# w2's four weight blocks asked for by ScalarE at 8 KB a row, in place of SyncE at 2 KB a piece

## The chip, the cores and the metric

One Trainium2 chip, one core. The metric is the device time of one execution in microseconds; three runs of the kernel before are at hand and one profiled execution. TensorE is the matmul engine (PE in the profile, PEld its weight loads), VectorE is DVE, ScalarE is ACT, GpSimd is POOL, and SyncE (SP, SPq for its DMA queue) issues transfers.

## What is computed

Cross attention over 32 sequences of 128 rows with 512 features, and then a feed-forward block with ternary weights (512 to 2048 and back), both with residuals. Cut to what matters:

```python
x = x + xattn(layernorm(x), ctx, mask)      # scores, softmax, readout with ctx
h = layernorm(x)
# bitlinear: xq = act_quant(rms_norm(h)); wq = weight_quant(w); xq @ wq.T + b
def weight_quant(w):
    scale = 1.0 / clip(mean(abs(w)), 1e-05)
    return clip(round(w * scale), -1, 1) / scale
h = gelu(silu(bitlinear(h, w1, b1)))         # 128 x 2048 for each sequence
h = layernorm(h) * g + b
x = x + bitlinear(h, w2, b2)                 # w2: 512 x 2048
```

The scale of a weight matrix is the mean of the absolute values of the whole of it, so w2 must have landed completely before any of it can be rounded, and all of it is needed for the first second product.

## The kernel before, in words

The work is cut into 32 tiles t of 128 rows (one sequence each). Every engine has one program written out by hand as a list of steps, and semaphores tie them together; an engine does its steps strictly in the order of its list. For each tile: SyncE loads x, ctx and both transposed (256 KB each, rows of 2 KB); TensorE makes scores, turns the probabilities and makes the readout; VectorE adds the readout to x; POOL centres and rounds it to fp16 (round_q1, L1575); SyncE turns it with a DMA transpose (transpose_q1, L253 to L257); TensorE makes first_product(t, h) in two halves h (L614 to L631); ScalarE applies silu (L1193) and gelu (L1202) and sums squares; VectorE applies gain and beta; POOL rounds; SyncE transposes again (transpose_q2); TensorE makes second_product (L633); VectorE adds it to x; SyncE stores. Tiles follow one another some six steps apart, so that all engines work on different tiles at a time.

The weights are prepared once, at the start. w1 lies raw in the first four of the eight buffers of hid, w2 in the last four (w2raw, L124): block c is 128 partitions by 2048 floats. The buffers are used by tiles 4 to 7 first, so silu(4) to silu(7) wait until their block has been rounded. For each block c of w2 ScalarE sums the absolute values of one half (weight_sum, L1139) and VectorE those of the other half (L1858). VectorE adds the eight half-sums of wsum up (wtot, L1868), TensorE adds over the partitions (weight_total, L546), VectorE makes the scale (L1870), and then POOL and ScalarE round the blocks into w2q (L1542, L1151), which VectorE clamps (L1893).

The transfers of w2 are asked for by SyncE in load_w2 (L249). w2T is the transposed weight, 2048 x 512, in DRAM, and block c takes four runs of 128 of its rows, so each partition gets four pieces of 2 KB. SyncE's list in this stretch reads (L317 to L332): transpose_q1(0), ctxT(6), ctx(3), **w2(0)**, ctxT(7), x(6), **w2(1)**, transpose_q1(1), **w2(2)**, **w2(3)**, x(7), xT(6), ctx(4), ctx(5), transpose_q1(2). transpose_q1(t) waits for POOL's round_q1(t), and all that is listed behind it waits too. load_ctx(t) waits for readout(t - 2).

```python
            def transpose_q1(t):
                sp.wait_ge(s_q1, t + 1)
                wait(sp, s_z[0], t - 3)
                wait(sp, s_z[1], t - 3)
                sp.dma_start(q1T[:, t % 4, :, :], q1[:, t % 3, :], transpose=True).then_inc(s_q1T[t % 4], 16)
```

ScalarE's list in this stretch (L1241 to L1263): exp_scores(3), copy_b1, round_w1(2), copy_probT(3), mean_term(4), square_x1(2), mean_term(5), exp_scores(4), square_x1(3), weight_sum(1, 0), exp_scores(5), copy_b2, silu(0, 0), copy_probT(4), weight_sum(1, 1), mean_term(6), silu(0, 1), weight_sum(1, 2), copy_probT(5), silu(1, 0), weight_sum(1, 3), silu(1, 1), gelu(0). copy_b1 reads what TensorE's turn_b1 (L551) left.

TensorE's list (L679 to L718): turn_b1, readout(2), turn_b2, warm(5), column_sums(4), turn_probs(3), turn_factors(0), warm(6), readout(3), warm(7), scores(4), which waits for mean_term(5), warm(8), scores(5), turn_probs(4), which waits for exp_scores(4), first_product(0, 0), column_sums(6), first_product(0, 1), turn_factors(1), turn_probs(5), first_product(1, 0), first_product(1, 1), weight_total(1), readout(4). warm(i) are six matmuls on zeros (L539 to L544). VectorE's list has weight_sum(1, 0) to (1, 3) between other steps, and then weight_sums_total(1), x_stats(7), weight_scale(1) (L2057 to L2070).

Of the kernel before, what the change touches and what calls it, by code (L numbers as in the profile page):

```python
# [15 lines left out]
P = 128  # L16
# [22 lines left out]

def build(nc, x_in, xT_in, ctx_in, ctxT_in, mask_in, w1T_in, b1_in, g_in, b_in, w2T_in, b2_in, out):  # L40
    NT, _, D = x_in.shape
    FF = w1T_in.shape[1]
    DC = D // P
    FC = FF // P
    HALF = FF // 2
    CH = 512
# [23 lines left out]
    with ExitStack() as stack:  # L70
# [3 lines left out]
        def sem(name):  # L74
            return stack.enter_context(nc.semaphore(name))
# [48 lines left out]
        w2raw = hid[:, 4:8, 0:FF]  # L124
# [34 lines left out]
        s_w2 = [sem(f"w2_landed{c}") for c in range(4)]  # L159
# [41 lines left out]
        def wait(eng, semaphore, value):  # L201
            if value > 0:
                eng.wait_ge(semaphore, value)
# [12 lines left out]
        def w2_flat(c):  # L216
            return w2q[:, 4 * c:4 * c + 4, :].rearrange("p a d -> p (a d)")
# [5 lines left out]
        def _(sp):  # L223
            def load_x(t):
                if t >= XR:
                    sp.wait_ge(s_out[t % XR], landed(t - XR, XR))
                sp.dma_start(xs[:, t % XR, :], x_in[t, :, :]).then_inc(s_x[t % XR], 16)
# [5 lines left out]
            def load_ctxT(t):  # L233
                wait(sp, s_score, t - CT + 1)
                wait(sp, s_csp, (t - CT) // 2 + 1)
                sp.dma_start(ctxT[:, t % CT, :, :], ctxT_in[t, :, :, :]).then_inc(s_ctxT[t % CT], 16)

            def load_ctx(t):
                wait(sp, s_read, t - CX + 1)
                sp.dma_start(ctx[:, t % CX, :], ctx_in[t, :, :]).then_inc(s_ctx[t % CX], 16)  # L240
# [5 lines left out]
            def load_w1(c):  # L246
                sp.dma_start(w1raw[:, c, :], w1T_in[c * P:(c + 1) * P, :]).then_inc(s_w1[c], 16)

            def load_w2(c):  # L249
                sp.dma_start(w2raw[:, c, :].rearrange("p (c d) -> p c d", d=D),  # L250
                             w2T_in[c * CH:(c + 1) * CH, :].rearrange("(c p) d -> p c d", p=P)).then_inc(s_w2[c], 16)

            def transpose_q1(t):  # L253
                sp.wait_ge(s_q1, t + 1)
                wait(sp, s_z[0], t - 3)
                wait(sp, s_z[1], t - 3)
                sp.dma_start(q1T[:, t % 4, :, :], q1[:, t % 3, :], transpose=True).then_inc(s_q1T[t % 4], 16)  # L257
# [59 lines left out]
            transpose_q1(0)  # L317
            load_ctxT(6)
            load_ctx(3)
            load_w2(0)  # L320
            load_ctxT(7)
            load_x(6)
            load_w2(1)
            transpose_q1(1)
            load_w2(2)
            load_w2(3)
            load_x(7)
            load_xT(6)
            load_ctx(4)
# [806 lines left out]

        @block.scalar
        def _(act):
            def weight_sum(k, c):  # L1139
                raw, s_landed = (w1raw, s_w1) if k == 0 else (w2raw, s_w2)  # L1140
                act.wait_ge(s_landed[c], 16)
                n = FF if c in WHOLE[k] else HALF
                unread = (w1q[:, c, :] if k == 0 else w2_flat(c))[:, 0:n]
                act.activation(unread, raw[:, c, 0:n], ACT.Abs, accum_out=wsum[:, k, c:c + 1]).then_inc(s_wsum[k], n // HALF)

            def round_w1(q):
                act.wait_ge(s_wsc[0], 1)
                cols = slice(q * CH, (q + 1) * CH)
                act.activation(w1q[:, :, cols], w1raw[:, :, cols], ACT.Identity, scale=wscale[:, 0:1]).then_inc(s_w1q[q], 1)
# [5 lines left out]
            def copy_b1():  # L1155
                act.wait_ge(s_bturn[0], 1)
                act.wait_ge(s_zero, 2)
                act.activation(rows1[0:ROWS, :], b1_ps, ACT.Copy).then_inc(s_rows[0], 1)
# [6 lines left out]
            def exp_scores(t):  # L1165
                wait(act, s_pTp, t - 3)
                act.wait_ge(s_centred, t + 1)
                act.activation(prob[:, t % 4, :], score[:, t % 4, :], ACT.Exp, bias=nbias[:, t:t + 1],
                               scale=-1.0, accum_out=psum_p[:, t:t + 1]).then_inc(s_prob, 1)

            def mean_term(t):

                act.wait_ge(s_csp, t // 2 + 1)
                act.wait_ge(s_mv1, t + 1)
                wait(act, s_centred, t - CR + 1)
                act.activation(corr[:, t % CR, :], csum_ps[:, t % 2 * P:(t % 2 + 1) * P], ACT.Identity,
                               scale=mv1[:, t, 0:1]).then_inc(s_corr, 1)

            def copy_probT(t):
                act.wait_ge(s_pTp, t + 1)  # L1180
                wait(act, s_read, t - 1)
                act.activation(probT[:, t % 2, :], probT_ps, ACT.Copy).then_inc(s_turn, 1)  # L1182

            def square_x1(t):
                if t == 0:
                    act.wait_ge(s_const, 1)
                act.wait_ge(s_xc, t + 1)
                wait(act, s_sq2, t)

                act.activation(junk_x[:, :], xc[:, t % 3, 0:D + 2], ACT.Square, scale=ROOT1,  # L1190
                               accum_out=sq2[:, t:t + 1]).then_inc(s_sq2, 1)
# [33 lines left out]
            mean_term(0)  # L1225
            mean_term(1)
            weight_sum(0, 0)
            exp_scores(0)
            copy_probT(0)
            exp_scores(1)  # L1230
            mean_term(2)
            copy_probT(1)
            mean_term(3)
            weight_sum(0, 1)
            weight_sum(0, 2)
            weight_sum(0, 3)
            exp_scores(2)
            square_x1(0)
            copy_probT(2)
            square_x1(1)  # L1240
            exp_scores(3)  # L1241
            copy_b1()
            round_w1(2)
            copy_probT(3)
            mean_term(4)
            square_x1(2)
            mean_term(5)
            exp_scores(4)
            square_x1(3)
            weight_sum(1, 0)  # L1250
# [1240 lines left out]
```

## Time and profile before

| | us |
|---|---|
| median of 3 runs (lowest, highest) | 420.21 (418.86, 420.68) |
| profiled execution, its own time | 419.71 |
| its span | 417.9 |
| busy: TensorE matmuls, ScalarE, VectorE, POOL | 385.4, 381.7, 365.9, 274.7 |
| DMA: all transfers | 73.87 MB, 64.7% of 16 engines' span in SyncE's queue |
| w2: four transfers of 1024 KB, median from issue to landing | 7.9 |

Busy time is the sum of an engine's instructions; an idle engine costs something only where it is on the chain that sets the end. In the page's slices DMA moves 274 to 411 GB/s in the first 63 us (six slices) and mostly 50 to 250 after. All plain loads and transposes are issued by SyncE, in one queue.

### The profile page before, as it was taken

To read this page: it belongs to the slowest core of one execution; us is meant where nothing else is said; L and a number is where in the kernel's file an instruction comes from. 1 tells how busy PE (TensorE), PEld (TensorE's weight loads), DVE (VectorE), ACT (ScalarE), POOL (GpSimd) and SP (SyncE) were. 2 spreads that over 40 slices of the span, in tenths; PEclk is the share of its full clock that TensorE was granted. 3 is DMA by queue.
4 is the path that set the end of the run, shared out by engine and by line. 5 is a ranking of instruction groups with operands and counts; after the bars stand their busy time and mean duration, and the time that the engine had idled before them with its cause. 6 is when DMAs were issued, how large, how long until landed. Compare 5 with 4: busy or idle time off the path is not lost.

```text
span 417.9 us, 6814 instructions
## 1 busy us (share of the span) xinstructions
PE 385.4 (92%) x1878; PEld 205.5 (49%) x1878; DVE 365.9 (88%) x571; ACT 381.7 (91%) x517; POOL 274.7 (66%) x373
## 2 busy tenths in 40 slices
PE   3999987899999999999999999999999987899896
PEld 2677353544455544544545455554545433444342
DVE  5278579989999989999999999989998689999992
ACT  1496999999999999999999999999999999999960
POOL 6358488774687838664785569499368855477930
PEclk9999998699999999999999999999999996999999
DMA  7999991556665787658568766594654423083484
GB/s 274 411 343 303 368 340 50 163 152 143 202 151 134 183 188 191 138 168 199 152 169 248 191 166 160 190 217 118 176 129 105 91 63 63 2 201 102 88 214 128
DMA packets 110389, 73.87 MB, mean 177 GB/s; under 512 B 87048, under 2 KB 87056, under 8 KB 109584
## 3 DMA queue, kind: packets, MB, share of 16 engines
q1 hardware_dynamic: 110352, 73.43, 64.7%
q8 instruction: 16, 0.26, 0.3%
q14 instruction: 21, 0.17, 0.1%
HBM read 44.05 MB, written 8.39 MB: 125 GB/s over the span
## 4 chain that ended last, share of the span: by engine, by line
issue 24%; PE 21%; ACT 20%; DVE 16%; POOL 13%; DMA 4%; DVEq 0%; POOLq 0%; SPq 0%; ACTq 0%
ACT junk_v L1211 6%; PE z L624 6%; DVE hid L1971 5%; DVE hid L1980 5%; PE acc L649 5%; ACT hid L1206 4%; ACT hid L1200 3%; POOL hid L1617 3%; DMA xT<-in_xT_dram 3%; PE ba L574 3%; PE ba L585 3%; POOL rstd L1606 2%; PE bb L599 2%; PE z L629 2%; ACT junk_l L1222 1%
## 5 line engine op out<-in xcount | busy, mean ns | idle before, releaser
L624 PE MATMUL z<-w1q,q1T 128*128 128x512 f16 x512 | 124.2, 386 | 2.8 <-ACT hid L1200 2.6
L649 PE MATMUL acc<-w2q,q2T 128*128 128x512 f16 x512 | 117.3, 379 | 0.4 <-DMA q2T<-hid 0.4
L1980 DVE SCALAR_TENSOR_TENSOR hid<-hid,rstd,beta 128x2048 f32<-128x2048 f32 x32 | 76.6, 2396 | 6.2 <-POOL rstd L1606 5.8
L624 PEld LDWEIGHTS z<-w1q,q1T 128*128 128x128 f16 x512 | 49.8, 99 | 65.2 <-ACT hid L1200 9.4
L1971 DVE SCALAR_TENSOR_TENSOR hid<-hid,nmu,gain 128x2048 f32<-128x2048 f32 x32 | 79.1, 2472 | 0.4 <-POOL nmu L1598 0.3
L649 PEld LDWEIGHTS acc<-w2q,q2T 128*128 128x128 f16 x512 | 49.9, 98 | 58.1 <-DMA q2T<-hid 0.9
L1985 DVE TENSOR_REDUCE am<-hid 128x1 f32<-128x2049 f32 x32 | 72.5, 2269 | 0.1
L1200 ACT ACTIVATE hid<-z,fac 128x1024 f32<-128x1024 f32 x64 | 70.7, 1118 | 0.9 <-PE z L629 0.5
L1222 ACT ACTIVATE junk_l<-hid 128x2050 bf16<-128x2050 f32 x32 | 61.1, 1910 | 3.8 <-DVE hid L1980 3.7
L1211 ACT ACTIVATE junk_v<-hid,gsum 128x2048 bf16<-128x2048 f32 x32 | 63.7, 1990 | 0.1
L1617 POOL TENSOR_SCALAR hid<-hid,kq 128x2048 f16<-128x2048 f32 x30 | 60.9, 2031 | 4.3 <-DVE kq L1992 2.7
L1206 ACT ACTIVATE hid<-hid 128x2048 f32<-128x2048 f32 x32 | 60.9, 1905 | 0.2
L629 PE MATMUL z<-rows,brows 128*128 128x512 bf16 x128 | 38.5, 383 | 1.4 <-DVE brows L1960 1.4
L1575 POOL TENSOR_SCALAR q<-xc,kq 128x512 f16<-128x512 f32 x32 | 36.0, 1124 | 4.9 <-DVE kq L1933 3.0
L574 PE MATMUL ba<-ctxT,xT 128*128 128x128 f32 x256 | 37.8, 293 | 0.4 <-DMA xT<-in_xT_dram 0.4
L585 PE MATMUL ba<-ctxT,neg 128*128 128x256 f32 x128 | 32.3, 398 | 6.1 <-DMA ctxT<-in_ctxT_dram 5.9
L599 PE MATMUL bb<-ctx,probT 128*128 128x512 f32 x64 | 34.0, 613 | 0.8 <-ACT probT L1182 0.5
L1568 POOL TENSOR_TENSOR rho<-sq,c_neghalf 128x2 f32<-128x2 f32 (+1 forms) x17 | 17.1, 1005 | 26.7 <-ACT junk_x L1190 26.7
L574 PEld LDWEIGHTS ba<-ctxT,xT 128*128 128x128 f32 x256 | 32.8, 201 | 3.1 <-issue 1.5
L585 PEld LDWEIGHTS ba<-ctxT,neg 128*128 128x128 f32 x128 | 24.8, 199 | 12.1 <-issue 7.3
L1921 DVE SCALAR_TENSOR_TENSOR xs<-bb,rsum,xs 128x512 f32<-128x512 f32 x32 | 23.8, 744 | 6.5 <-PE bb L599 6.2
L1604 POOL TENSOR_SCALAR ve<-vsum 128x2 f32<-128x2 f32 (+1 forms) x18 | 9.9, 548 | 28.8 <-ACT junk_v L1211 28.4
(105 smaller groups left out, 573.3 us busy)
## 6 DMA issues: line engine op xcount, KB each, us to landing
ctxT<-in_ctxT_dram SPq DMA_DIRECT2D x32, 256.0 KB, 3.7
xs<-in_x_dram SPq DMA_DIRECT2D x32, 256.0 KB, 3.9
xT<-in_xT_dram SPq DMA_DIRECT2D x32, 256.0 KB, 3.5
ctx<-in_ctx_dram SPq DMA_DIRECT2D x32, 256.0 KB, 3.5
out_dram<-xs SPq DMA_DIRECT2D x32, 256.0 KB, 3.1
hid<-in_w1T_dram SPq DMA_DIRECT2D x4, 1024.0 KB, 10.0
hid<-in_w2T_dram SPq DMA_DIRECT2D x4, 1024.0 KB, 7.9
gain<-in_g_dram SPq DMA_DIRECT2D x1, 1024.0 KB, 11.1
```

The costliest lines, as they stand in the source:

```text
L574: mm = pe.matmul(score_ps, xT[:, t % XT, c, :], ctxT[:, t % CT, c, :], start=False, stop=(c == DC - 1))
L585: mm = pe.matmul(csum_ps, neg[:, :], ctxT[:, t % CT:t % CT + 2, c, :], start=(c == 0), stop=(c == DC - 1))
L624: pe.matmul(z_ps[h][:, c * CH:(c + 1) * CH], q1T[:, t % 4, k, :], w1q[:, k, f0:f0 + CH], start=(k == 0), stop=False)
L649: mm = pe.matmul(a, q2T[:, t % 2, c, :], w2q[:, c, :], start=False, stop=(c == FC - 1))
L1200: act.activation(hid[:, t % HR, half(h)], z_ps[h][:, :], ACT.Silu, scale=fac[:, t, 0:1]).then_inc(s_silu[h], 1)
L1206: act.activation(hh, hh, ACT.Gelu, accum_out=gsum[:, t:t + 1]).then_inc(s_gelu, 1)
L1211: act.activation(junk_v[:, :], hid[:, t % HR, 0:FF], ACT.Square, bias=gsum[:, t:t + 1], scale=-float(FF), accum_out=vsum[:, t:t + 1]).then ...
L1222: act.activation(junk_l[:, :], hid[:, row_of(t), 0:FF + 2], ACT.Square, scale=ROOT2, accum_out=ysum[:, t:t + 1]).then_inc(s_sq, 1)
L1617: pool.tensor_scalar(q2_of(t), hid[:, row_of(t), 0:FF], kq2[:, t:t + 1], UNIT, ALU.mult, ALU.mult).then_inc(s_q2, 1)
L1971: dve.scalar_tensor_tensor(out=hid[:, row_of(t), 0:FF], in0=hid[:, t % HR, 0:FF], scalar=nmu[:, t:t + 1], in1=gain[:, :], op0=ALU.add, op1 ...
L1980: dve.scalar_tensor_tensor(out=hh, in0=hh, scalar=rstd[:, t:t + 1], in1=beta[:, :], op0=ALU.mult, op1=ALU.add).then_inc(s_l, 1)
L1985: dve.tensor_reduce(am2[:, t:t + 1], hid[:, row_of(t), 0:FF + 1], AX_X, ALU.max, apply_absolute_value=True).then_inc(s_am2, 1)
```

## The change

load_w2 moves from SyncE's program to ScalarE's, and the host lays w2T out otherwise, so that a partition's 2048 floats of a block lie together in DRAM: a row of 8 KB. What lands in w2raw is the same. SyncE's list loses its four load_w2; in ScalarE's list load_w2(0) stands behind exp_scores(3), load_w2(1) behind round_w1(2), and load_w2(2) and load_w2(3) behind mean_term(5). No wait is added or removed.

```diff
-            def load_w2(c):
-                sp.dma_start(w2raw[:, c, :].rearrange("p (c d) -> p c d", d=D),
-                             w2T_in[c * CH:(c + 1) * CH, :].rearrange("(c p) d -> p c d", p=P)).then_inc(s_w2[c], 16)
...
             load_ctx(3)
-            load_w2(0)
             load_ctxT(7)
             load_x(6)
-            load_w2(1)
             transpose_q1(1)
-            load_w2(2)
-            load_w2(3)
             load_x(7)
...
         def _(act):
+            def load_w2(c):
+                act.dma_start(w2raw[:, c, :], w2T_in[c * P:(c + 1) * P, :]).then_inc(s_w2[c], 16)
+
...
             exp_scores(3)
+            load_w2(0)
             copy_b1()
             round_w1(2)
+            load_w2(1)
             copy_probT(3)
             mean_term(4)
             square_x1(2)
             mean_term(5)
+            load_w2(2)
+            load_w2(3)
             exp_scores(4)
...
-        "w2T": np.asarray(inputs["L0_ffn_w2"]).T,
+        "w2T": np.asarray(inputs["L0_ffn_w2"]).T.reshape(4, FF // 4 // P, P, D).transpose(0, 2, 1, 3).reshape(4 * P, FF // 4 // P * D),
```

## Rows read from the trace of the kernel before

**Rows 1.** ScalarE's windows: stretch, length, busy, granted clock, DMA share, GB/s.
```profile
36.00:100.00 64.00, 62.93 (x92) 0.92 0.73 218
...
300.00:400.00 100.00, 98.86 (x115) 0.97 0.44 98
```

**Rows 2.** TensorE's timeline: start, duration, engine, line, operation, [idle before, releaser].
```profile
24.64 1.13 PE L574 MATMUL ba<-ctxT,xT 128*128 128x128 f32 x8 [0.40 <-DMA xT<-in_xT_dram]
...
32.28 1.02 PE L599 MATMUL bb<-ctx,probT 128*128 128x512 f32 x2
...
33.79 0.22 PE L570 MATMUL ba<-maskb,ones_b 128*128 128x128 bf16 x1
...
42.94 1.89 PE L624 MATMUL z<-w1q,q1T 128*128 128x512 f16 x8
...
47.95 0.35 PE L549 MATMUL acc<-wtot,neg 128*128 128x1 f32 x2 [0.43 <-DVE wtot L1868]
...
68.82 0.23 PE L570 MATMUL ba<-maskb,ones_b 128*128 128x128 bf16 x1 [1.86 <-ACT corr L1176]
...
77.17 3.48 PE L624 MATMUL z<-w1q,q1T 128*128 128x512 f16 x8
```

**Rows 3.** Timeline of ScalarE.
```profile
27.79 1.87 ACT L1158 ACTIVATE rows<-z 9x2048 bf16<-9x2048 bf16 x1 [0.54 <-PE z L555]
...
31.77 0.28 ACT L1182 ACTIVATE probT<-bb 128x128 f32<-128x128 f32 x1 [0.22 <-PE bb L593]
...
35.45 0.40 ACT L1168 ACTIVATE prob<-score,nbias 128x129 f32<-128x129 f32 x1 [2.23 <-DVE nbias L1909]
...
45.46 1.11 ACT L1200 ACTIVATE hid<-z,fac 128x1024 f32<-128x1024 f32 x1
...
47.42 0.19 ACT L1144 ACTIVATION_READ_ACCUMULATOR w2q<-hid 128x1 f32 x1
```

**Rows 4.** Windows, all engines; the last columns are DMA share and GB/s.
```profile
17.00:20.00 3.00, 2.42 (x10) 1.60 (x9) 2.21 (x8) 1.09 (x5) 0.96 (x3) 1.00 1.02 427
...
33.00:36.00 3.00, 3.00 (x26) 2.54 (x25) 2.70 (x8) 0.77 (x4) 2.41 (x5) 1.00 1.07 391
...
37.20:40.30 3.10, 3.10 (x16) 2.09 (x15) 3.10 (x7) 2.43 (x6) 3.10 (x2) 1.00 0.76 118
```

**Rows 5.** Waits of VectorE (36-60 us), ScalarE (100-418): total, times, longest.
```profile
DVE wsum L1862 <- DMA hid<-in_w2T_dram: 2.6, 2, 1.6
...
ACT junk_l L1222 <- DVE hid L1980: 3.7, 6, 2.4
```

**Rows 6.** SyncE's queue: timeline, then line 250's four issues in ns.
```profile
28.83 0.43 SPq L250 DMA_DIRECT2D hid<-in_w2T_dram  x1
...
36.42 1.20 SPq L257 DMA_TRANSPOSE q1T<-q  x1
...
37.67 1.13 SPq L250 DMA_DIRECT2D hid<-in_w2T_dram  x2
...
L250 SPq DMA_DIRECT2D hid<-in_w2T_dram x4: 434/470/582, 27.3 to 38.3; - x4
```

**Rows 7.** Issue to landing: w2(1), q1T(1), then w2(2) and w2(3) together.
```profile
DMA to landing us min/median/max: 10.3/10.3/10.3
...
DMA to landing us min/median/max: 3.9/3.9/3.9
...
DMA to landing us min/median/max: 5.7/6.8/8.0
```

**Rows 8.** Timeline of VectorE.
```profile
47.64 0.16 DVE L1868 TENSOR_REDUCE wtot<-wsum 128x1 f32<-128x8 f32 x1
...
53.62 0.35 DVE L1909 CUSTOM_DVE_ANT_0 score<-corr,ba,nrs 128x128 f32<-128x128 f32 x1 [2.26 <-PE ba L574]
```

**Rows 9.** DMA packets of 37 to 39.2 us.
```profile
DMA packets 635, 0.30 MB, mean 134 GB/s; under 512 B 558, under 2 KB 558, under 8 KB 634
```

**Rows 10.** Window of all engines; granted clock is third from the right.
```profile
72.00:78.00 6.00, 4.73 (x19) 3.30 (x20) 5.95 (x14) 5.97 (x8) 5.48 (x7) 0.50 0.25 64
```

## The prediction

> **What bounds the kernel now.** I read the windows of ScalarE first. From 36 to 100 us it is busy for 62.93 of 64 us, and from 300 to 400 us for 98.86 of 100 [rows 1], so in that time the end is set by the sum of ScalarE's own instructions: a change counts there only if it shifts ScalarE's start or gives it work. Before that the chain of waits lies on TensorE. In its timeline the reader sees no idle time in brackets between 24.64 us (released by xT) and 47.95, where 0.43 us of idle end, so it worked without a gap to 47.52 [rows 2]. It hands over to ScalarE at the first products: silu(1, 0) starts at 45.46 [rows 3], when the product that began at 42.94 and took 1.89 us [rows 2] has added its two bias matmuls. So what moves TensorE between 27 and 47 us moves the whole rest; what moves only VectorE, POOL or DMA in that time does nothing until it reaches TensorE or ScalarE.
>
> DMA looks like a limit too: at 33 to 36 us it moves 391 GB/s with its engines busy throughout [rows 4]. But the only wait for w2 that the profile names is VectorE's: 2.6 us in two times [rows 5].
>
> **The change, part by part.**
>
> *1. w2 lands earlier: worth nothing.* In the old order w2(2) and w2(3) stand in SyncE's program behind transpose_q1(1), which waits for round_q1(1) and issues at 36.42; the pair follows at 37.67 [rows 6] and lands 5.7 and 8.0 us after its issues [rows 7], the second at 46.3. In the new order ScalarE asks for them after mean_term(5), which ended 2.23 us before 35.45, at 33.2 [rows 3]: some 4 us earlier. VectorE's two sums then need not wait. But the next step, wtot at 47.64 [rows 8], needs all eight half-sums, and ScalarE's last one is read out at 47.42 plus 0.19, so 47.61 [rows 3]. It stands behind silu(1, 0), which has nothing to do with w2. So w2's scale comes at the same time, and with it the roundings. Gain: 0.
>
> *2. 8 KB rows in place of 2 KB pieces.* While w1 (8 KB rows) was most of the traffic, 427 GB/s were moved; in the stretch of w2 and x, all in 2 KB pieces, 391 [rows 4]. For w2's 4.19 MB that is 9.8 us of DMA time against 10.7, 0.9 less. Nothing on the path waits for that time, so it pays 0; it only shortens the backlog in term 4. [...]
>
> *3. Four issues on ScalarE.* The trace has no DMA issued by ScalarE. The nearest rows are SyncE's: its four issues of w2 took 0.43 to 0.58 us, and the longest issue near them, the transpose's, 1.20 [rows 6]. The lower bound is 0, if the issue hides beside the instruction before it; nothing below that, since ScalarE loses no instruction. I take 0.5, by the same transfer on the other queue. load_w2(0) stands before copy_b1, which started at 27.79 after 0.54 us of idle time, released by TensorE [rows 3]: 0.54 covers 0.5. load_w2(1) stands before copy_probT(3), which started at 31.77 after 0.22 of idle time [rows 3]; 0.28 is left. readout(3) on TensorE needs probT. It started at 32.28 after warming matmuls [rows 2], while probT was ready at 31.77 + 0.28 = 32.05; now it is ready at 32.33, and with a hand-over of some 0.05 TensorE is 0.1 late. mean_term(5) then ends at 33.5, before scores(4), which waits for it, at 33.79 + 0.1 [rows 2]. load_w2(2) and (3) take 33.5 to 34.5, and exp_scores(4) is not before 35.45 [rows 3]; without that cover they would cost their 1.0 in full. **Cost 0.1.** At 1.20 each: the first overruns its cover by 0.7, the second by 1.0, so probT(3) is ready at 33.7 and TensorE 1.5 late; the last two end near 37.3, and exp_scores(4) is still through before turn_probs(4) wants it. Upper end 1.5.
>
> *4. q1T(1) beside w2.* first_product(1, 0) waits for this transfer. It is issued at 36.42 [rows 6] and lands 3.9 us later, at 40.3 [rows 7]; the product starts at 42.94 without having waited [rows 2]: a slack of 2.6 us. Until now only w2(1) was ahead of it, landed at 28.83 + 10.3 = 39.1 [rows 6, 7]. Now w2(2) and w2(3), 2.1 MB, are in flight from ScalarE's queue on the same engines. Lower bound: the queues share by bytes, q1T(1) keeps most of its slack, 0 late. Upper bound: all of w2 goes first. w2(0) and (1) gain 0.5 by the faster rate, so 38.6; 2.1 MB at 427 GB/s are 4.9, so 43.5; the transpose itself needs about 1.3 more, the better part of the 2.2 us window that holds its packets, 558 small ones in all [rows 9]: 44.8, which is 1.9 late. Between these: the packets alternate. q1T(1) has 512 packets of 256 B, 32 on each of 16 engines; w2(2) and (3) have 16 rows on each, at 8 KB / 26.7 GB/s = 0.31 us. When the transpose arrives, near 37.6, some 14 rows are left: 4.3 us, in which 14 of the 32 go by. The other 18 take 0.5 us and the completion some 0.7: 43.1. I take that, **0.2 late**: it is the case between ends that no row tells apart. [...]
>
> *5. SyncE's queue without w2.* x(7), xT(6), ctx(4) and ctx(5) are issued 1.1 us earlier, since the pair's issues took 1.13 [rows 6], and 2.1 MB no longer stand ahead of them. From 37.2 to 40.3 us DMA moved only 118 GB/s [rows 4]: the transpose ran, and w2(2) was only being started. That hole fills. The first user of these four is readout(4), on TensorE behind 47.52, after the hand-over to ScalarE: 0.
>
> Sum: 0 + 0 + 0.1 + 0.2 + 0 = +0.3. The profiled execution took 419.71 (a span of 417.9 and 1.8 around it), so it would take 420.0. It lies 0.5 below the median of the three runs, 420.21; on that scale the forecast is **420.5**. A measurement of this kernel tells about 0.5% (2.1 us) from no change, and 0.3 lies well within.
>
> **The rivals.**
>
> *A. The transpose starves and TensorE's clock falls (slower).* Place: TensorE at 42.94. [...] The products (1, 0) and (1, 1), both on the path, would cost 1.6 more each: 420.2 + 1.9 + 3.2 = **425.3**. Against: TensorE had not waited for 18 us before 42.94, and 44.8 needs nearly all of w2 ahead. It decides from a landing after 45.0, or from a fall of the clock near 43: 0.12.
>
> *B. Issues on ScalarE are dear.* At 1.20 each +1.5, with term 4 +1.7: **421.9**, within 0.5%. For: it is that queue's first use, beside SyncE's issues until 29.3. Against: none of SyncE's plain w2 issues took over 0.58. 0.08, a quarter of it over the bound.
>
> *C. VectorE's head start reaches the end (faster).* The 2.6 us of waits go, and ScalarE's longest wait for VectorE, late in the kernel, is 2.4 [rows 5]. If all of that went: 420.2 - 2.4 = **417.8**. Against: behind its sums VectorE stops at wtot for ScalarE anyway, and soon after it waits 2.26 us for TensorE until 53.62 [rows 8], so the lead is eaten by then. 0.12.
>
> *D. The change does not do what it says.* w2 in the other queue is served no sooner and no faster, the issues hide, and q1T(1) is on time. Every term is 0: **420.2**. 0.12.
>
> **How the numbers follow.** Forecast 0.56, A 0.12, B 0.08, C 0.12, D 0.12. Same: 0.56 + 0.12 + 0.06 = 0.74. Slower: 0.12 + 0.02 = 0.14. Faster: 0.12. Both upper ends together (1.5 + 1.9) make 423.6; I take 422.7, as they seldom meet. To leave out no more than 2 in 10, the range must take in C, with A left out: 417.7 to 422.7. The likeliest case alone, with the spread of the three runs (418.86 to 420.68), would be 418.9 to 421.5.
>
> **What the changed profile should show.** Four issues on ScalarE's queue near 27.3, 31.6 and 33.5 us, each near 0.5; copy_probT(3) at about 32.0; w2(3) landed at 42 to 43.5, not 46.3; no wait of VectorE for w2, but wtot still at 47.6 to 48; q1T(1) landed at 41 to 43.5, not 40.3; silu(1, 0) at 45.5 to 45.9, and the old timeline behind it, shifted by that. DMA in 37.2 to 40.3 us well above 118 GB/s. The forecast is wrong if silu(1, 0) moves by more than 2 us either way, if the clock drops near 43 us, or if silu(1, 0) stays and the end still moves: then a chain after 48 us counts that I hold to be only shifted.

## The result, and the profile after

The changed kernel is slower, where no measurable difference was forecast.

| | before | after |
|---|---|---|
| median (lowest to highest), 4 runs each | 419.56 (418.86 to 420.68) | 426.94 (425.92 to 428.08) |
| ratio of the two, 95% interval | | 1.0177 [1.0157, 1.0197] |
| profiled execution, and its span | 419.71, 417.9 | 426.55, 424.7 |

426.94 lies outside the range of 417.7 to 422.7. The page of the changed kernel, parts 2 and 3 (q1 is the queue in which SyncE asks, q10 that of ScalarE):

```profile
span 424.7 us, 6814 instructions
...
PEclk9996999999999999999999999999999997999999
...
q1 hardware_dynamic: 108240, 69.24, 61.1%
q10 hardware_dynamic: 576, 4.19, 2.5%
```

All 4.19 MB of w2 now run in q10. TensorE's clock has a dent in the fourth slice, 32 to 42 us. TensorE's timeline there, with the columns of [rows 2]:

```profile
23.65 1.13 PE L566 MATMUL ba<-ctxT,xT 128*128 128x128 f32 x8 [0.55 <-DMA xT<-in_xT_dram]
...
30.57 0.82 PE L536 MATMUL z<-idle 128*128 128x256 bf16 x6
37.09 2.04 PE L591 MATMUL bb<-ctx,probT 128*128 128x512 f32 x2 [5.70 <-DMA ctx<-in_ctx_dram]
38.93 1.49 PE L536 MATMUL z<-idle 128*128 128x256 bf16 x6
40.21 0.31 PE L562 MATMUL ba<-maskb,ones_b 128*128 128x128 bf16 x1
40.31 1.50 PE L566 MATMUL ba<-ctxT,xT 128*128 128x128 f32 x8
...
49.80 1.89 PE L616 MATMUL z<-w1q,q1T 128*128 128x512 f16 x8
```

The reader is to see the 5.70 in brackets: readout(3) waited for **ctx(3)**, a transfer that the prediction never looked at. Before, readout(3) ran at 32.28 without a wait [rows 2]. SyncE's queue in the changed kernel shows the issue, and the view of line 240 from 25.6 to 26 us the time to its landing:

```profile
25.16 0.52 SPq L236 DMA_DIRECT2D ctxT<-in_ctxT_dram  x1
25.72 0.43 SPq L240 DMA_DIRECT2D ctx<-in_ctx_dram  x1
...
DMA to landing us min/median/max: 11.1/11.1/11.1
```

Before, the same two views gave

```profile
26.86 0.43 SPq L240 DMA_DIRECT2D ctx<-in_ctx_dram  x1
...
DMA to landing us min/median/max: 4.3/4.3/4.3
```

so ctx(3) landed at 31.2, 1.1 us before readout(3) wanted it. The chain of work that ended last now runs through this transfer:

```profile
25.72 11.13 DMA ctx<-in_ctx_dram
36.85 0.24 issue
37.09 2.04 PE bb L591 x2
```

**Where the time went.** This run reached scores(3) at 23.65, before at 24.64 [rows 2]. That 0.99 us lies ahead of the first changed issue, so I count from scores(3). readout(3) starts 13.44 us after it (before 32.28 - 24.64 = 7.64): 5.80 later. From readout(3) to first_product(1, 0), at 49.80, it is 12.71 us (before 42.94 - 32.28 = 10.66): 2.05 more. These 2.05 are the matmuls at the low clock (0.57 in 36 to 42 us): readout(3) took 2.04 where it took 1.02 [rows 2], the six warming matmuls 1.49 against 0.82, scores(4) 1.50 against 1.11. The last, before:

```profile
33.85 1.11 PE L574 MATMUL ba<-ctxT,xT 128*128 128x128 f32 x8
```

Together 7.85, less the head start of 0.99: 6.86. Windows of all engines (columns as in [rows 4], the granted clock third from the right):

```profile
31.40:37.10 5.70, 0.01 (x1) 0.04 (x1) 0.88 (x2) 0.75 (x3) 1.24 (x3) 0.75 0.99 396
36.00:42.00 6.00, 4.91 (x21) 3.30 (x22) 1.51 (x4) 0.00 (x0) 1.75 (x3) 0.57 0.83 341
42.00:48.00 6.00, 6.00 (x36) 4.15 (x34) 5.28 (x15) 5.02 (x11) 4.99 (x8) 1.00 0.63 185
```

In the first row TensorE does nothing, while DMA moves 396 GB/s: the wait is not a lack of transfer, but of the one transfer that counts. Then comes a clock of 0.57 (0.50 in [rows 10]), and from 42 us on one of 1.00.

ScalarE's timeline (ACTq is its queue of issues):

```profile
25.22 0.38 ACTq L1132 DMA_DIRECT2D hid<-in_w2T_dram  x1
25.72 0.39 ACT L1163 ACTIVATE prob<-score,nbias 128x129 f32<-128x129 f32 x1
26.74 1.87 ACT L1153 ACTIVATE rows<-z 9x2048 bf16<-9x2048 bf16 x1 [0.54 <-PE z L547]
26.75 0.33 ACTq L1132 DMA_DIRECT2D hid<-in_w2T_dram  x1
28.52 1.99 ACT L1144 ACTIVATE w1q<-hid,wscale 128x2048 f16<-128x2048 f32 x1
30.72 0.28 ACT L1177 ACTIVATE probT<-bb 128x128 f32<-128x128 f32 x1 [0.21 <-PE bb L585]
31.27 0.82 ACTq L1132 DMA_DIRECT2D hid<-in_w2T_dram  x2
42.30 0.40 ACT L1163 ACTIVATE prob<-score,nbias 128x129 f32<-128x129 f32 x1 [10.14 <-DVE nbias L1908]
...
52.22 1.11 ACT L1195 ACTIVATE hid<-z,fac 128x1024 f32<-128x1024 f32 x1
```

exp_scores(4) waited 10.14 us where it waited 2.23, and silu(1, 0) starts at 52.22, before at 45.46 [rows 3]: +6.76. I followed ScalarE's later table loads to the end (ACT_TABLE_LOAD in the trace, 1.28 us each, at its exp, silu and gelu; every kernel here has 17, 17 and 13 of them on the same three steps): each of the 47 is 6.7 to 6.9 us late, and the span is 6.8 longer. So all of the loss arises between 31 and 43 us, and nothing is won back or lost behind it.

**Why ctx(3) was late.** The packets of 29 to 31 us, by queue (packets, MB, share), in the changed kernel:

```profile
DMA packets 159, 0.83 MB, mean 413 GB/s; under 512 B 0, under 2 KB 0, under 8 KB 79
...
q10 hardware_dynamic: 79, 0.65, 77.9%
q1 hardware_dynamic: 79, 0.16, 21.3%
```

and in the kernel before, same stretch:

```profile
q1 hardware_dynamic: 381, 0.71, 102.0%
```

The queues got the same number of packets, 79 each, but one of q10 is an 8 KB row and one of q1 a 2 KB row: the bytes are split four to one. SyncE's queue fell from 0.71 MB in 2 us (w2's own pieces included) to 0.16. Everything in it suffered: ctxT(6) took 8.5 us (before 4.2), ctxT(7) 13.7 (8.0), x(6) 16.2 (8.3). Of these, ctx(3) had the least slack.

### The profile page after: what moved, and what is told of

Read it like the earlier page. It is cut to its first block, busy times and chain, and to the rows that moved or that the text cites. A ratio compares the mean times of both kernels' runs of the same rounds, so it can differ in the third digit from the quotient of the medians.

```text
span 424.7 us, 6814 instructions
## 1 busy us (share of the span) xinstructions
PE 381.4 (90%) x1878; PEld 203.3 (48%) x1878; DVE 366.1 (86%) x571; ACT 381.6 (90%) x517; POOL 269.7 (64%) x373
## 3 DMA queue, kind: packets, MB, share of 16 engines
q10 hardware_dynamic: 576, 4.19, 2.5%
## 4 chain that ended last, share of the span: by engine, by line
issue 23%; ACT 21%; DVE 20%; PE 19%; POOL 9%; DMA 4%; SPq 2%; DVEq 0%; POOLq 0%; ACTq 0%
ACT junk_v L1206 6%; DVE hid L1979 6%; DVE hid L1970 5%; PE z L616 5%; PE acc L641 5%; ACT hid L1201 4%; ACT hid L1195 4%; PE ba L566 3%; POOL hid L1616 3%; DMA ctx<-in_ctx_dram 3%; DVE am L1984 2%; PE bb L591 2%; POOL rstd L1605 2%; PE z L621 1%; DVE st L1898 1%
## 5 line engine op out<-in xcount | busy, mean ns | idle before, releaser
L616 PE MATMUL z<-w1q,q1T 128*128 128x512 f16 x512 | 122.6, 383 | 3.7 <-ACT hid L1195 3.7
L566 PE MATMUL ba<-ctxT,xT 128*128 128x128 f32 x256 | 36.2, 285 | 1.6 <-DMA xT<-in_xT_dram 1.6
L1574 POOL TENSOR_SCALAR q<-xc,kq 128x512 f16<-128x512 f32 x32 | 33.8, 1057 | 4.9 <-DVE kq L1932 3.0
L1920 DVE SCALAR_TENSOR_TENSOR xs<-bb,rsum,xs 128x512 f32<-128x512 f32 x32 | 23.8, 743 | 12.9 <-PE bb L591 12.8
L566 PEld LDWEIGHTS ba<-ctxT,xT 128*128 128x128 f32 x256 | 31.5, 194 | 4.3 <-issue 2.9
L1561 POOL TENSOR_SCALAR xc<-xs,sum 128x512 f32<-128x512 f32 x32 | 26.2, 818 | 9.9 <-DVE xs L1920 9.5
L577 PEld LDWEIGHTS ba<-ctxT,neg 128*128 128x128 f32 x128 | 24.8, 199 | 12.9 <-issue 8.2
L1567 POOL TENSOR_TENSOR rho<-sq,c_neghalf 128x2 f32<-128x2 f32 (+1 forms) x17 | 13.7, 804 | 26.8 <-ACT junk_x L1185 26.8
```

Of the source, the lines that this page charges most:

```text
L566: mm = pe.matmul(score_ps, xT[:, t % XT, c, :], ctxT[:, t % CT, c, :], start=False, stop=(c == DC - 1))
L577: mm = pe.matmul(csum_ps, neg[:, :], ctxT[:, t % CT:t % CT + 2, c, :], start=(c == 0), stop=(c == DC - 1))
L616: pe.matmul(z_ps[h][:, c * CH:(c + 1) * CH], q1T[:, t % 4, k, :], w1q[:, k, f0:f0 + CH], start=(k == 0), stop=False)
```

## The experiments

My theory behind the result: the two queues take turns by packets (79 to 79 in 29 to 31 us), so the 8 KB rows in the second queue (0.65 MB) starve the 2 KB transfers of the first (0.16 MB); the wait of 5.70 us for ctx(3) does the rest, with the clock of 0.57 behind it. The rivals: it is the second queue as such, whatever its rows (E1); it is the 8 KB rows as such (E2); the fall of the clock is the greater part of it (E5). Each group ran beside the kernel before on the same chip, whose median was 419.57 for E1 to E4, 419.53 for E5 to E8, 419.28 for E9 to E11 and 419.50 for E12. The ratios are made from runs taken in the same rounds, so they can differ by 0.1 or 0.2% from the quotient of two medians.

**E1. ScalarE's queue and places, but the old layout in 2 KB pieces.**

```diff
-                act.dma_start(w2raw[:, c, :], w2T_in[c * P:(c + 1) * P, :]).then_inc(s_w2[c], 16)
+                act.dma_start(w2raw[:, c, :].rearrange("p (c d) -> p c d", d=D),
+                              w2T_in[c * CH:(c + 1) * CH, :].rearrange("(c p) d -> p c d", p=P)).then_inc(s_w2[c], 16)
```

> The changed kernel, w2 still asked for by ScalarE at the same places, but in pieces of 2 KB as before. Theory P (the two queues take turns packet by packet, so a queue of 2 KB rows gets a fifth of the bytes beside one of 8 KB rows): with equal pieces SyncE's queue gets half, ctx(3) lands near 32 us instead of 36.8, readout(3) waits some 0.6 us instead of 5.7, and the time is +0.3 to +1.5 us on the kernel before. Rival V (w2 is simply asked for too early, its 1 to 2 MB stand ahead whatever their rows): ctx(3) still lands after 35 us and the time stays at +6 to +8.

Measured: 424.08 (423.52 to 425.56), ratio 1.0091 [1.006, 1.0122]. ctx(3) landed 8.1 us after its issue. TensorE's timeline:

```profile
36.51 2.05 PE L591 MATMUL bb<-ctx,probT 128*128 128x512 f32 x2 [2.71 <-DMA ctx<-in_ctx_dram]
```

The wait is 2.7 and not 0.6, and the clock fell here as well (2.05); the time is 4.5 us above the kernel before, three times the upper end of my expectation and below that of the rival. So the rows carry part of the loss. A good half stays without them. It can't be put down to the second queue alone, since w2 is asked for early here too: w2(0) at 27.60, ahead of ctx(3) at 28.21, while in the kernel before w2(0) stood behind ctx(3). E6 takes the second queue away. The packets by queue in this kernel, first 30 to 33 us, then 33.5 to 36:

```profile
q10 hardware_dynamic: 401, 0.82, 74.6%
q1 hardware_dynamic: 162, 0.30, 27.8%
...
q10 hardware_dynamic: 260, 0.50, 53.7%
q1 hardware_dynamic: 255, 0.46, 49.8%
```

From 33.5 us on the queues got nearly the same number of packets, with equal rows and so nearly equal bytes (0.50 and 0.46 MB). Before that SyncE's queue, which had just come out of the transpose of q1(0), got less than its half (162 of 563 packets). Why is open; my expectation had the fair half throughout. (The profiled execution took 425.56, 1.5 above the median.)

**E2. SyncE's queue and old places, but 8 KB rows.** (The host layout is that of the change.)

```diff
-                sp.dma_start(w2raw[:, c, :].rearrange("p (c d) -> p c d", d=D),
-                             w2T_in[c * CH:(c + 1) * CH, :].rearrange("(c p) d -> p c d", p=P)).then_inc(s_w2[c], 16)
+                sp.dma_start(w2raw[:, c, :], w2T_in[c * P:(c + 1) * P, :]).then_inc(s_w2[c], 16)
```

> The kernel before with only the layout changed: SyncE asks for w2 at the old places, at 8 KB a row. Theory P: in one queue nothing takes turns, ctx(3) lands as before (near 31 us), w2(1) some 0.5 to 0.9 us sooner, nothing on the path moves: -0.3 to +0.5 us. Rival R (8 KB rows hold the engines up by themselves): +3 or more.

Measured: 419.57 (10 runs), ratio 0.9988 [0.9969, 1.0006]. ctx(3) took 4.4 us and nothing waited for it. VectorE's waits for w2 sank from 2.6 [rows 5] to

```profile
DVE wsum L1861 <- DMA hid<-in_w2T_dram: 1.5, 2, 1.2
```

and the end did not move. By themselves, in SyncE's queue and places, the 8 KB rows were harmless and worth nothing here. The gain in rate of term 2 is not clear either. w2(0) and w2(1) landed 7.8 and 10.3 us after their issues, before 7.9 and 10.3; w2(2) and w2(3) took 5.0 and 6.9, before 5.7 and 8.0. From 33 to 36 us DMA moved 394 GB/s, before 391 [rows 4], and from 31.5 to 35.5 us 419, before 389.

**E3. The changed kernel, with w2(0) and w2(1) asked for behind mean_term(4).**

```diff
             exp_scores(3)
-            load_w2(0)
             copy_b1()
             round_w1(2)
-            load_w2(1)
             copy_probT(3)
             mean_term(4)
+            load_w2(0)
+            load_w2(1)
```

> The changed kernel with load_w2(0) and (1) moved behind mean_term(4), so that they are issued near 31 us and not at 25.2 and 26.8. Theory P: ctx(3), ctxT(6), ctxT(7) and x(6) are through before w2 begins, readout(3) does not wait; next q1T(1) takes turns with w2 and lands near 42.5, some 0.6 after it is wanted: 0 to +1.5 us. Rival I (issuing on ScalarE costs by itself, wherever it stands): +5 or more.

Measured: 423.78 (421.76 to 424.61), ratio 1.0083 [1.0055, 1.0111]. ctx(3) took 5.8 us, and readout(3) waited 0.30. (w2 was asked for at 32.13, so it was not beside ctx(3). Why that took 1.5 us longer than before is open, and shows how much such a landing can vary.) So this loss went, and the next one came, far larger than the 0.6 that I expected: q1T(1), issued at 37.16, took 9.1 us, and first_product(1, 0) waited for it:

```profile
46.39 3.36 PE L616 MATMUL z<-w1q,q1T 128*128 128x512 f16 x8 [2.47 <-DMA q1T<-q]
```

Eight matmuls that take 1.89 took 3.36: the clock fell, to 0.58 in 46.4 to 50 us. This is rival A, place and mechanism, with the low clock over one product and not two. ScalarE's issues, asked for where nothing covers them, also left 0.52 us of idle time here; exp_scores(4) behind them waited 2.19 for VectorE anyway, so nothing shows that it reached the end:

```profile
33.10 0.63 ACT L1185 ACTIVATE junk_x<-xc 128x514 bf16<-128x514 f32 x1 [0.52 <-issue]
```

**E4. The changed kernel, with ctx(3) asked for earlier.**

```diff
             load_xT(5)
+            load_ctx(3)
             load_ctxT(5)
             load_x(5)
             transpose_q1(0)
             load_ctxT(6)
-            load_ctx(3)
```

> The changed kernel with load_ctx(3) moved up in SyncE's list, behind xT(5). Theory P: readout(3) no longer waits, but SyncE's queue is as starved as before: ctxT(7), x(6) and q1T(1) still land near 40, 43 and 44 us, wanted at 38, 38.6 and 42, and the wait comes back at column_sums(6) or at the first products: +3 to +5 us. Rival S (only ctx(3) was short of time, all else has slack): 0 to +1 us.

Measured: 422.01 (10 runs), ratio 1.0057 [1.0033, 1.0082]. readout(3) did not wait, and 4.9 of the 7.4 us are gone. The 2.4 that stay lie between the rival's 0 to 1 and my 3 to 5. This is the direct test: w2 runs as in the changed kernel, and only ctx(3) is out of its way. What is left shows as waits for the other transfers in SyncE's queue: x(6) landed 14.3 us after its issue, and VectorE waited 2.4 for it; q1T(1) took 7.4. TensorE's timeline:

```profile
43.87 1.89 PE L616 MATMUL z<-w1q,q1T 128*128 128x512 f16 x8 [0.46 <-DMA q1T<-q]
...
46.12 0.60 PE L621 MATMUL z<-rows,brows 128*128 128x512 bf16 x2 [0.36 <-DVE brows L1959]
```

**E5 and E10. The changed kernel, with eight more groups of warming matmuls before readout(3)**, so that the clock stays up during the wait. They write what nothing reads. E10 is E5 again.

```diff
             warm(6)
+            warm(6)
...
+            warm(6)
             readout(3)
```

> The changed kernel with eight more groups of six warming matmuls in front of readout(3), some 5.3 us of TensorE's time, which lie inside its wait of 5.7 us. [...] Rival: the matmuls after the wait are not on the path, or the clock falls all the same; then +6.5 to +8.

> The same kernel as in e5_warm. There the first product began 1.7 us earlier after its start than in the changed kernel, yet the time was not shorter. Theory (the clock's fall costs its 1.7 us): 1 to 2 us below e9_again. Rival (what is saved before 48 us is lost again later): within 0.7 us of e9_again, with ScalarE's lag on the kernel before growing after 100 us in the trace.

Measured: 427.27 (426.87 to 427.39), 1.0188 [1.016, 1.0215]; again 426.98 (424.93 to 429.93), 1.0188 [1.0153, 1.0223]. The clock stayed up, in E5 (1.00 from 31 to 38 us):

```profile
37.86 1.10 PE L591 MATMUL bb<-ctx,probT 128*128 128x512 f32 x2 [0.67 <-DMA ctx<-in_ctx_dram]
```

first_product(0, 0) came 18.18 us after the start of scores(3), 1.75 earlier than in the changed kernel. Yet the time, for which I had forecast 1.5 to 2.2 us below the changed kernel, did not shrink, and 7.7 above the kernel before lies in the rival's range. In that run ScalarE's lag behind the kernel before grew from 5.5 us to 6.5 by 278 us, in steps near 110 and 278 us. In E10 there was little to keep: ctx(3) itself took 12.9 us, readout(3) waited 2.28 behind the warming matmuls, and first_product(0, 0) came 20.26 us after scores(3), against 20.65 in E9; the lag then grew from 8.1 to 9.4. The lag of the changed kernel stays at 6.7 to 6.8, but E9's grew too, by 0.3 us, so not all of such growth belongs to the warming. The six times of E10 lie 5 us apart. What the fall of the clock costs in the end is therefore not settled: 2.05 us in the trace, nothing in the medians. That it is the greater part of the loss is refuted.

**E6. All in SyncE's queue at 8 KB, w2(0) and w2(1) moved ahead**, so that ctx(3) has w2 before it without any second queue.

```diff
             transpose_q1(0)
+            load_w2(0)
             load_ctxT(6)
             load_ctx(3)
-            load_w2(0)
+            load_w2(1)
             load_ctxT(7)
             load_x(6)
-            load_w2(1)
             transpose_q1(1)
```

> All of w2 in SyncE's queue at 8 KB a row, but asked for as early as ScalarE does it: w2(0) ahead of ctxT(6) and ctx(3), w2(1) behind ctx(3), (2) and (3) at the old places. Theory P (turn-taking between queues): one block ahead in one queue costs its own transfer time, 2.5 us; ctx(3) lands near 33.7 counted from the same start, readout(3) waits about 1.5 us, perhaps with a fall of the clock: +1.5 to +3.5. Rival V (the early request is the cost, in whichever queue): +6 or more.

Measured: 423.47 (422.25 to 423.74), ratio 1.0089 [1.0054, 1.0125]. ctx(3) took 7.2 us.

```profile
34.76 1.34 PE L598 MATMUL bb<-ctx,probT 128*128 128x512 f32 x2 [2.33 <-DMA ctx<-in_ctx_dram]
```

A loss needs no second queue: one block ahead of ctx(3) in its own queue gives a wait of 2.3 us, more than the 1.5 I expected, a fall of the clock (readout(3) took 1.34, before 1.02) and +3.9 us, a little above my +3.5. That is as much as E1 lost. So an early request alone accounts for about half of the 7.4 us, in either queue. The other half came only with the second queue and 8 KB rows together. It is a question of which bytes go ahead of ctx(3).

**E7. The changed kernel, in rows of 4 KB** (two pieces for each partition, and a host layout to suit).

```diff
-                act.dma_start(w2raw[:, c, :], w2T_in[c * P:(c + 1) * P, :]).then_inc(s_w2[c], 16)
+                act.dma_start(w2raw[:, c, :].rearrange("p (h d) -> p h d", d=2 * D),
+                              w2T_in[2 * c * P:2 * (c + 1) * P, :].rearrange("(h p) d -> p h d", p=P)).then_inc(s_w2[c], 16)
```

> The changed kernel with w2's rows cut into two pieces of 4 KB, asked for by ScalarE at the same places. Theory P: SyncE's 2 KB rows get a third of the bytes, between a half (2 KB pieces, readout(3) waited 2.7 us) and a fifth (8 KB rows, 5.7 us): a wait of 3.5 to 5 us and +5 to +7. Rival (the size of the pieces does nothing, 2.7 and 5.7 differ by chance of timing): a wait near 2.7 or near 5.7.

Measured: 424.75 (422.55 to 425.6), ratio 1.0121 [1.0082, 1.0161]. ctx(3) took 8.9 us. TensorE's timeline, and the packets of 31 to 35 us:

```profile
35.29 1.10 PE L591 MATMUL bb<-ctx,probT 128*128 128x512 f32 x2 [3.40 <-DMA ctx<-in_ctx_dram]
```

```profile
q10 hardware_dynamic: 278, 1.07, 67.9%
q1 hardware_dynamic: 272, 0.50, 33.4%
```

Equal counts once more, and bytes two to one. In the profiled execution, which took 422.55, 2.2 below the median, the clock did not fall in spite of a wait of 3.4 us (it was 1.00 in 31.9 to 35.3 us). With E1 and the changed kernel the row size makes a series: at 2, 4 and 8 KB ctx(3) took 8.1, 8.9 and 11.1 us, readout(3) waited 2.7, 3.4 and 5.7, and the ratios are 1.0091, 1.0121 and 1.0177. The step from 4 to 8 KB is clear. That from 2 to 4 KB is not: the two intervals overlap, and at 8 KB alone four traces gave 11.1, 11.3, 11.3 and 12.9 us.

**E8. w2(0) and w2(1) in SyncE's queue in their old places, w2(2) and w2(3) in ScalarE's, all at 8 KB.** SyncE gets a load_w2 of its own again. This leaves ctx(3) alone and gives q1T(1) the two blocks that the prediction feared.

```diff
             load_ctx(3)
+            load_w2(0)
             load_ctxT(7)
             load_x(6)
+            load_w2(1)
             transpose_q1(1)
...
             exp_scores(3)
-            load_w2(0)
             copy_b1()
             round_w1(2)
-            load_w2(1)
             copy_probT(3)
```

> Half of the change undone: w2(0) and (1) in SyncE's queue at the old places, at 8 KB a row; w2(2) and (3) asked for by ScalarE behind mean_term(5). Theory P: ctx(3) is on time, near 31 us, and readout(3) does not wait; but the transpose of q1T(1), 32 packets of 256 B on each engine, takes turns with the rows of w2(2) and (3) and lands near 43.5 to 44.5 instead of 40.3: first_product(1, 0) waits 0.5 to 2 us: +0.5 to +3. Rival S (only ctx(3) was short of time): -0.5 to +0.5.

Measured: 420.91 (420.57 to 421.5, 10 runs), ratio 1.0035 [1.0023, 1.0047]. ctx(3) took 4.6 us. q1T(1), issued at 36.18, took 8.1 (before 3.9 [rows 7]), so it landed at 44.3, as expected:

```profile
44.40 1.89 PE L621 MATMUL z<-w1q,q1T 128*128 128x512 f16 x8 [1.50 <-DMA q1T<-q]
```

**E9. The changed kernel once more**, beside another group.

> The changed kernel once more, as the base for the next one on the same chip: +6.5 to +8 us on the kernel before.

Measured: 426.87 (426.03 to 428.02), ratio 1.0173 [1.0151, 1.0195]; ctx(3) took 11.3 us, and readout(3) waited 5.95.

**E11. E8 with 2 KB pieces in both queues.** (The old host layout; ScalarE's load_w2 as in E1.)

```diff
             transpose_q1(1)
-            load_w2(2)
-            load_w2(3)
             load_x(7)
...
             mean_term(5)
+            load_w2(2)
+            load_w2(3)
             exp_scores(4)
```

> As e8_half, with all of w2 in pieces of 2 KB: w2(2) and (3) asked for by ScalarE behind mean_term(5). Theory P (one packet from each queue in turn): each of the 32 packets of q1T(1) on an engine now waits for a 2 KB piece, 0.08 us, and not for an 8 KB row, 0.31: q1T(1) lands near 41.7, before it is wanted, and the time is -0.5 to +0.6 on the kernel before, against +1.4 in e8_half. Rival (the transpose is held up by the bytes ahead, not by turns): q1T(1) still lands after 43 and +1 or more.

Measured: 421.58 (420.96 to 423.69), ratio 1.0046 [1.0028, 1.0064]. q1T(1), issued at 36.11, took 8.7 us, and here first_product(1, 0) was late and slow:

```profile
44.98 3.05 PE L622 MATMUL z<-w1q,q1T 128*128 128x512 f16 x8 [2.14 <-DMA q1T<-q]
```

My expectation failed. It counted only the turns of the transpose, but w2(1) stands before it in SyncE's own queue, and of the packets of 36 to 37.5 us below this queue got only half, 142 beside 141: w2(1) landed at 41.3, in E8 at 41.5, before at 39.1 [rows 6, 7]. (The profiled execution took 423.69, 2.1 above the median, so the matmuls at the low clock need not be in the median.) The packets of 36 to 37.5 us, then of 42.2 to 43:

```profile
q10 hardware_dynamic: 141, 0.29, 51.5%
q1 hardware_dynamic: 142, 0.29, 51.2%
...
q10 hardware_dynamic: 113, 0.23, 75.6%
q1 hardware_dynamic: 113, 0.03, 16.5%
```

The packets of 256 B (0.03 MB in 113) show up late, and then come one to one with the 2 KB pieces: for a sixth of the engines' time (16.5%) they are half of the packets.

**E12. The kernel before, with only xT(3) moved to ScalarE's queue**, behind exp_scores(0): can a second queue serve for what is urgent, and not for what is large? scores(3) waits 0.40 for this transfer [rows 2].

```diff
-            load_xT(3)
...
             exp_scores(0)
+            act.wait_ge(s_score, 1)
+            act.dma_start(xT[:, 0, :, :], xT_in[3, :, :, :]).then_inc(s_xT[0], 16)
             copy_probT(0)
```

> The kernel before, with only the load of xT(3) moved to ScalarE's queue, behind exp_scores(0). In SyncE's queue it stands behind three blocks of w1 and takes 11.9 us to land, and TensorE waits 0.40 us for it at 24.64. Theory P (queues take turns, so a small transfer alone in its queue passes the bulk): it lands within 3 to 5 us, before 18 us, and the wait of 0.40 is gone: -0.5 to +0.1 us. Rival (the engines serve in the order of the requests, whatever the queue): it still takes 10 us or more, and the time does not move.

Measured: 420.3 (12 runs), ratio 1.0017 [1.0001, 1.0033]. xT(3) landed in 6.5 us, before in 11.9, and the wait of 0.40 is gone. (I expected 3 to 5 us, and no loss.) But the last block of w1, which it overtook, landed at 24.5, before at 23.8, and ScalarE waited 0.49 and VectorE 0.81 for it, where neither waited before. VectorE's timeline:

```profile
24.58 1.22 DVE L1863 TENSOR_REDUCE wsum<-hid 128x1 f32<-128x1024 f32 x1 [0.81 <-DMA hid<-in_w1T_dram]
```

None of the versions beats the kernel before; E2 equals it.

## Why the prediction was wrong

**The step that failed** is the choice of transfer in term 4, "q1T(1) beside w2". The case that I took there fits what was measured: I let the packets alternate, 8 KB against the small ones, and in 29 to 31 us the queues got 79 each. But I applied it to one transfer only, the one that my reading of TensorE's list put next, and term 5 spoke only of what SyncE issues behind w2. ctx(3), ctxT(7) and x(6) are issued among w2(0) and w2(1), and I did not look up when they land and who wants them then. Even if w2(0) were issued at 27.3, as I had it, ctx(3) would have been in flight beside it. The same sum on ctx(3) would have warned: ctxT(6) and ctx(3) have 8 rows of 2 KB on each of 16 engines, and each of these 16 rows lets one of w2 go by, at 0.31 us (the term's own figure, 8 KB at a sixteenth of 427 GB/s), as long as w2 has one. With the issues where I had them only the 8 rows of w2(0) are there: 2.5 us late against 1.1 us of slack, a wait of 1.4, as an estimate. With the issues where they came (term 3) w2(1) follows: 5.0 us late, a wait of 3.9; 5.7 were measured, and 2.05 more went to matmuls at the low clock. So the transfer that I left out and the issue times that I had wrong failed together, and the sum by turns still falls 1.8 us short of the wait.

**Term 1 (0): right.** VectorE's waits for w2 went, and wtot waits for ScalarE's last half-sum. In VectorE's timeline after:

```profile
54.40 0.16 DVE L1867 TENSOR_REDUCE wtot<-wsum 128x1 f32<-128x8 f32 x1 [2.61 <-ACT w2q L1139]
```

It starts 6.76 later than before [rows 8], as late as all the rest.

**Term 2 (0): right at the end**, by E2, though the faster rate that it read from two windows did not show there for w2(0) and w2(1). **Term 3 (+0.1): right in that it cost next to nothing, wrong in its place.** The issues took 0.38, 0.33 and, the pair, 0.82 us, and ScalarE's idle time ahead of copy_probT(3) was 0.21 with them and 0.22 without: nothing was lost. But they ran ahead of ScalarE's instructions. I had them 2.7, 7.0 and 8.9 us after the start of scores(3) (27.3, 31.6 and 33.5 less 24.64); they came after 1.6, 3.1 and 7.6. So w2(1) stood 4 us earlier beside SyncE's transfers than I held. E3, with both blocks asked for late, cut the wait to 0.30.

**Term 4 (+0.2 for q1T(1)):** in the changed kernel it did not come to the test, because POOL's round_q1(1) was delayed too; q1T(1) was issued at 42.18, as w2 ended (w2(3) landed at 42.7), and took 3.0 us. Where the wait for ctx(3) was out of the way, it was undersized: I had a landing 6.7 us after the issue (43.1 less 36.42), and E4, E8 and E3 gave 7.4, 8.1 and 9.1. The 0.7 for the completion in its sum was my estimate, on no row; before, the last of the small packets ran at 39.3 to 39.4 us and q1T(1) landed at 40.3, some 0.9 to 1.0 behind it. E8 and E11 show a part of what the term lacked: w2(1), ahead of the transpose in its own queue, landed over 2 us later than before.

**Term 5 (0):** for the four transfers that it names nothing waited; the ones it leaves out decided.

**The rivals.** A (the starved transpose and the clock, 425.3) came true on another transfer: ctx(3) took 11.1 us, and a clock of 0.57 came behind the wait. The 1.6 that it adds for each product is 3.48 less 1.89 [rows 2], before, at a clock of 0.50 in 72 to 78 us [rows 10], some us behind a wait of 1.86 [rows 2]. E3 and E11 show it in its own place, q1T(1) landing 9.1 and 8.7 us after its issue and the product behind taking 3.36 and 3.05, so 1.5 and 1.2 more. B is refuted, since the longest of the four issues on ScalarE took 0.46 us and not 1.20. C is refuted: the waits went, and no table load of ScalarE came earlier for it. D is refuted by the landings.

On the length of a turn the trace of the changed kernel shows this: w2(0)'s 8 rows on each engine, one behind the other at the 0.31 us of term 4, would be through in 2.5 us. Its first packets ran between 27 and 28 us (7 of them, 0.06 MB), and it landed at 33.3, so they did not all go in one turn.

## What to carry to other kernels

Before a transfer moves to another queue, list everything in flight in the old queue over that time, with each landing and the moment at which its first user wants it: the one with the least slack decides, not the one next on the list. A second queue was here not more bandwidth (from 31.4 to 37.1 us 396 GB/s, before 386) but another order, and where both queues had work its share of the bytes went mostly by the size of its rows (0.65 MB beside 0.16 at 8 KB against 2 KB, 1.07 beside 0.50 at 4 KB, 0.50 beside 0.46 at 2 KB). Bulk that nobody waits for yet did best behind the urgent transfers in the same queue (E2 against E6 and the changed kernel). If a TensorE wait of some microseconds can arise, look at the granted clock behind it as well (here 0.57 behind 5.70 us).

## What the runs showed that I had not expected

- Two queues got nearly equal counts of packets in most stretches, whatever their size: 79 to 79 (8 KB and 2 KB), 278 to 272 (4 KB and 2 KB), 260 to 255 (2 KB both), 113 to 113 (2 KB and 256 B). There are exceptions that no run explains: 401 to 162 at the start in E1, 85 to 33 from 30 to 31 us in E7, and, with SyncE's queue ahead, 106 to 46 from 34 to 35 us in the changed kernel.
- DMAs that ScalarE asks for were issued before the instructions listed ahead of them had run: w2(0) at 25.22, while exp_scores(3), listed ahead of it, started at 25.72; w2(1) at 26.75, while round_w1(2), listed ahead, started at 28.52. The description ahead of the prediction, by which an engine does its steps strictly in the order of its list, does not hold for these issues. w2(1) came 0.01 us after the start of copy_b1, which had waited 0.54, and E3's first issue 0.08 us after that of copy_probT(3), which had waited 0.21. So in these two cases the issue came when the wait ahead of it in the list had ended, and before the work ahead of it was done; no run tests this by itself.
- The clock fell after TensorE's waits of 5.70, 2.71 and 2.33 us before readout(3) (the matmuls took 2.04, 2.05 and 1.34, where they take 1.02 to 1.10), but not after 3.40 us in E7's profiled execution, nor after 2.28 us in E10's, where 6.06 us of warming matmuls had gone before. The length of the wait alone does not tell.
- Keeping the clock up during the wait won 1.75 us at first_product(0, 0) in E5 and 0.4 against E9 in E10, and nothing at the end in either. Where E5's gain was given back is only in part seen (1.0 us between 105 and 278 us).
